# A two-block image kernel on one core: 64-channel halves on 128 partitions, decays further ahead, carry copies on GpSimd

## The reference, cut to what matters

```python
x = x + L0(_gn(x))      # B, C, H, W = 16, 192, 32, 32
x = x + L1(_gn(x))
# L0: projection to z (384), x (384), B, C (32 each), dt (12); depthwise 3x3 convolution and silu on x, B, C;
#     chunked scan (8 chunks of 128 tokens, 12 heads of 32) with att = (C B^T) * exp(cumsum) * dt;
#     layer norm, times z, output projection
# L1: projection to x_in (192), delta (192), B, C (16 each); softplus of delta; selective scan over 1024 tokens:
h = jnp.exp(d_t[..., None] * A) * h + (d_t * x_t)[..., None] * b_t[:, None, :]
y_t = jnp.einsum('bdn,bn->bd', h, c_t)
#     y + D * x_in, output projection
```

## Time and profile before

| | us |
|---|---|
| median of 3 runs | 3382.27 (3380.13 to 3385.87) |
| the profiled execution | 3382.05, span 3380.3 |
| TensorE busy | 2844.2 (84%) |
| VectorE busy | 2711.6 (80%) |
| ScalarE busy | 1929.9 (57%) |
| GpSimd busy | 1593.6 (47%) |
| granted TensorE clock, mean | 0.92 of full |

### The profile page before, as it was taken

One profiled execution on the slowest core, in us unless ns is written; L12 is line 12 of the kernel. 1 busy time (PEld: TensorE's weight loads), 2 busy tenths in 40 slices (PEclk: granted clock), 3 DMA queues, 4 the chain that ended last, 5 costly groups with the idle time before them and its releaser, 6 DMA issues. The chain is left out here.

```text
span 3380.3 us, 62242 instructions
## 1 busy us (share of the span) xinstructions
PE 2844.2 (84%) x20640; PEld 1502.5 (44%) x20640; DVE 2711.6 (80%) x4364; ACT 1929.9 (57%) x4507; POOL 1593.6 (47%) x1235
## 2 busy tenths in 40 slices
PE   3788888988888898888888888898888988888865
PEld 2554536353453634445354453544445354443510
DVE  1357979789697978979689797978969798797997
ACT  1637475564657547475664746547475664746542
POOL 2114545454454545545355444545545455554555
PEclk8989999899999989999899989989999999989976
DMA  2132141422314142241423215142241424214131
GB/s 52 25 99 70 60 139 49 131 73 86 97 54 137 54 129 78 68 123 54 120 73 106 82 50 140 51 141 73 74 109 54 119 73 123 79 58 128 42 113 59
DMA packets 104163, 290.97 MB, mean 86 GB/s; under 512 B 25373, under 2 KB 27020, under 8 KB 103820
## 3 DMA queue, kind: packets, MB, share of 16 engines
q1 hardware_dynamic: 103820, 286.71, 28.5%
HBM read 181.84 MB, written 39.85 MB: 66 GB/s over the span
## 5 line engine op out<-in xcount | busy, mean ns | idle before, releaser
L754 POOL TENSOR_TENSOR hc<-hst,bcrep 128x512 f32<-128x512 f32 x768 | 1202.0, 1565 | 1155.8 <-DVE hst L1249 1127.6
L1298 PE MATMUL bank<-hc,sel 128*32 128x512 f32 x1536 | 435.4, 650 | 113.3 <-POOL hc L754 109.5
L1236 DVE TENSOR_TENSOR wr<-durep,bcrep 128x512 f32<-128x512 f32 x768 | 520.1, 677 | 2.9 <-DMA bcrep<-bc_rows 2.9
L1249 DVE TENSOR_TENSOR_SCAN hst<-dec,wr 128x512 f32<-128x512 f32 x256 | 396.0, 1547 | 99.0 <-ACT carry L991 71.2
L842 ACT ACTIVATE ssd<-bank,ncs 128x128 f32<-128x128 f32 x1536 | 438.3, 385 | 48.7 <-PE bank L1298 47.0
L1298 PE MATMUL bank<-xna,wt0a 128*128 128x128 f32 (+3 forms) x1088 | 303.5, 381 | 46.0 <-DVE xnb L1056 27.6
L1249 DVE TENSOR_TENSOR_SCAN hst<-bank,carry,wr 128x512 f32<-128x512 f32 x240 | 306.4, 1277 | 22.7 <-ACT bank L950 13.3
L950 ACT ACTIVATE bank<-durep,aneg 128x512 f32<-128x512 f32 x368 | 251.3, 687 | 121.0 <-DVE hst L1249 63.3
L1298 PE MATMUL bank<-ssd,wcv 64*32 64x512 f32 (+1 forms) x6144 | 307.6, 543 | 0.0
L950 ACT ACTIVATE dec<-durep,aneg 128x512 f32<-128x512 f32 x400 | 290.3, 731 | 6.4 <-DVE hst L1249 4.7
L1298 PE MATMUL bank<-xnb,wt0b 128*128 128x128 f32 (+3 forms) x1088 | 289.3, 368 | 0.0
(11 more groups left out here) (189 smaller groups left out, 4975.3 us busy)
## 6 DMA issues: line engine op xcount, KB each, us to landing
durep<-scratch SPq DMA_DIRECT2D x192, 512.0 KB, 3.8
bcrep<-bc_rows SPq DMA_DIRECT2D x128, 512.0 KB, 4.9
ssd<-stage SPq DMA_DIRECT2D x384, 140.4 KB, 2.9
ssd<-bcst SPq DMA_DIRECT2D x128, 74.4 KB, 2.7
xa<-in_x_dram SPq DMA_DIRECT2D x16, 512.0 KB, 4.1
scratch<-u SPq DMA_DIRECT2D x32, 256.0 KB, 2.1
scratch<-delta SPq DMA_DIRECT2D x32, 256.0 KB, 2.5
out_dram<-x1a SPq DMA_DIRECT2D x16, 512.0 KB, 4.8
```

What stands on the lines that cost most here:

```text
L754: nc.gpsimd.tensor_tensor(hc[:, i % CRING, :], hst[:, i % HRING, :], bcrep[:, g, 1, :], ALU.mult).then_inc(hc_ready.sem, 1)
L1236: nc.vector.tensor_tensor(wr[:, i % WRING, :], durep[:, j % SLOTS_DU, 1, :], bcrep[:, g, 0, :], ALU.mult).then_inc(w_made.sem, 1)
L1249: nc.vector.tensor_tensor_scan(hst[:, i % HRING, :], decay_of(i), wr[:, i % WRING, :], carry[:, g:g + 1] if hf else 0.0, ALU.mult, ALU.add ...
L1298: return nc.tensor.matmul(out, lhsT, rhs, start=start, stop=stop, skip_group_check=True)
```

## The change

- **Halves on 128 partitions.** `xb`, `xnb` and `x1b` are 128 x 512 instead of 64 x 1024: the first half of the tokens on partitions 0 to 63, the second on 64 to 127. Weights for them are held twice. A pair of halves is then two matmuls over the first 128 channels and two of 64 rows each. One bn_stats goes for each set of statistics, and normalisation has half the elements a partition. `gb` is doubled and halved in value. The gate uses weights with zero rows (`wtz`).
- **Fills.** dt is projected with B and C (76 columns). VectorE adds the bias from the bank into `dtt`, TensorE turns it with four transposes (`step_lengths`), ScalarE copies it into `dtx`. Fills are eight, made in pairs.
- **Projections.** Both halves of a piece together, in slots 40 to 43, in the order dA, BC, xA, xdB; biases are added in ScalarE's copies (`p1b`).
- **Decays** are made two units further ahead up to unit 11 and one further ahead behind it; of the first eight, four have their home in SBUF.
- **Carry copies** go to GpSimd, behind the product with C. The dt additions stand behind VectorE's scan in slot 2.

```diff
-FILL_AT = (0, 0, 1, 1, 1, 1, 2, 2, 2)
-FILL_COPY_AT = (0, 0, 1, 1, 2, 2, 2, 3, 3)
+FILL_AT = (0, 0, 1, 1, 1, 1, 2, 2)
+FILL_COPY_AT = (0, 0, 1, 1, 2, 2, 3, 3)
-P1_AT = (4, 4, 5, 7, 7, 8, 9, 10)
+P1_AT = (4, 5, 6, 7)
+FRONT_UNITS, LEAD_UNITS = 8, 12
 def decay_bank(i):
-    if i < 8 or i >= 38:
+    if i < FRONT_UNITS:
+        return (0, 1, None, None)[i % 4]
+    if i >= 38:
         return i % 2
     return 6 + i % 2 if 31 <= i < 36 else None
+def decays_made(s):
+    return min(max(min(s + 3, LEAD_UNITS), s + 2), UNITS)
...
# GpSimd, states_by_c
+                if hf == 0:
+                    nc.gpsimd.tensor_copy(carry[:, i:i + 1], hst[:, i % HRING, HALF - 1:HALF]).then_inc(carried.sem, 1)
...
# ScalarE
+                if s == 3:
+                    act.wait_ge(dt_ps.sem, dt_ps.at(n, 1))
+                    by_half = bank[B_DT][:, :].rearrange("p (c h k) -> p h c k", c=CPH, h=2)
+                    for h in range(2):
+                        ins = nc.scalar.copy(dtx[:, h * CPH:(h + 1) * CPH, :], by_half[:, 1 - h, :, 0:NH])
+                    ins.then_inc(dtx_ready.sem, 1)
...
-                        decay(b, s, end, first)
+                        for i in range(decays_made(s - 1) if s else 0, decays_made(s)):
+                            decay(b, i, end, first)
...
-                        if 2 <= s < HU + 2:
-                            act.wait_ge(scanned.sem, scanned.at(b, s - 1))
-                            nc.scalar.copy(carry[:, s - 2:s - 1], hst[:, (s - 2) % HRING, HALF - 1:HALF]).then_inc(carried.sem, 1)
...
# VectorE, first_block_later
+                if s == 2:
+                    dve.wait_ge(fill_ps.sem, fill_ps.at(n, 6))
+                    for h in range(2):
+                        nc.vector.tensor_scalar(dtt[(1 - h) * CB_:(1 - h) * CB_ + NH, :], bank[FILL_BANKS[(4 + h) % 3]][2 * NS:2 * NS + NH, :],
+                                                dtb[2 * NS:2 * NS + NH, :], None, ALU.add).then_inc(dtt_ready.sem, 1)
...
# TensorE, fill
+                m, h = FILL_TILES[k]
+                c0, w = DI + m * P, P if m < XM else 2 * NS + NH
+                ps = [bank[FILL_BANKS[(k + h) % 3]] for h in range(2)]
+                for h in range(2):
+                    if k + h >= 3:
+                        pe.wait_ge(fill_copied.sem, fill_copied.at(n, k + h - 2))
+                    if k + h == 7:
+                        pe.wait_ge(dtt_ready.sem, dtt_ready.at(n, 1))
+                    mm(ps[h][0:w, :], wt0a[:, c0:c0 + w], xna[:, h * HALF:(h + 1) * HALF], True, False)
+                for h in range(2):
+                    rows = slice(h * CB_, (h + 1) * CB_)
+                    mm(ps[h][0:w, :], wt0b[rows, m * P:m * P + w], xnb[rows, :], False, True).then_inc(fill_ps.sem, 1)
+            def step_lengths(n):
+                pe.wait_ge(dtt_ready.sem, dtt_ready.at(n, 2))
+                pe.wait_ge(fill_copied.sem, fill_copied.at(n, 6))
+                for c in range(CPH):
+                    ins = nc.tensor.transpose(bank[B_DT][:, c * P:(c + 1) * P], dtt[:, c * Q:(c + 1) * Q], ident[:, :])
+                ins.then_inc(dt_ps.sem, 1)
...
# TensorE, conv
                 if u == 1:
+                    pe.wait_ge(dtx_ready.sem, dtx_ready.at(n, 1))
                     pe.wait_ge(fill_copied.sem, fill_copied.at(n, FILLS))
```

More of the change, by code:

```diff
@@ L94 @@
 MID = 1
-P1_TILES = (("dA", 0), ("BC", 0), ("xA", 0), ("xdB", 0), ("xdB", 1), ("dA", 1), ("xA", 1), ("BC", 1))
-K_BC, K_XA, K_MID, K_D2, K_X2 = 2, 3, 5, 6, 7
+P1_PIECES = ("dA", "BC", "xA", "xdB")
+P1_TILES = [(what, h) for what in P1_PIECES for h in range(2)]
+BIAS = {"dA": 0, "xdB": 1, "xA": 2, "BC": 3}
+K_D2, K_BC, K_XA, K_X2, K_MID = 2, 3, 5, 6, 8
 K_ALL = len(P1_TILES)
@@ L678, in _ @@
             made_before(nc.gpsimd.memset(mv[:, :, :], 0.0))
-            for t in stage + [bcst]:
+            for t in stage + bcst:
                 made_before(nc.gpsimd.memset(t[:, :], 0.0))
@@ L1630 @@
 EXP_LN = "natural_log_exp_and_others"
-NLOADS = 76
-PREPS = 12
+NLOADS = 79
+PREPS = 14
 DVE_STEPS = 35
```

251 lines of the change are left out of this document (128 added, 123 removed).

## The result

| | before | after |
|---|---|---|
| median | 3384.07 (4 runs, 3380.13 to 3385.88) | 3324.36 (4 runs, 3319.02 to 3333.08) |
| span of the profiled execution, us | 3380.3 | 3318.1 |
| TensorE busy, us | 2844.2 | 2745.2 |
| VectorE busy, us | 2711.6 | 2732.5 |
| ScalarE busy, us | 1929.9 | 1935.1 |

The ratio of after to before is 0.9828, with a 95% interval of 0.9801 to 0.9855, so 1.7% faster. The forecast was 3324.0. Three single executions that took far longer than the others of their kernel (3668.86 us of the kernel before, 5344.23 and 10289.23 in two of the experiments) are left out of all ratios and medians.

The account below looks back on a forecast made before the run. Bound: a chain along TensorE in the front, a ring through all engines in the chunk stage. From 3382.05 us, -73 - 9 + 22 - 4 + 6 = -58 gave 3324 us; 8 in 10 from 3283 to 3385.

Parts of the forecast that it names:

- The front: Normalisation to first convolution falls from 23.7 to 18.2 us, set by VectorE's dtt addition: net 73 us gained.
- The extra cost: Last matmuls before the first convolution at the lower clock in half the passes, 1.7 us each: 13 us lost.
- The sign that the prediction named: First convolution 18 to 19 us after normalisation in every pass, TensorE waiting ahead of it for VectorE's dtt addition.
- Rows to attention: Rows of chunk 0 to its attention: VectorE is ready when the chunk comes, 0.6 us a pass, 9 us gained.
- The 22.3 us: VectorE's waits for ScalarE's decays before the change, 1.4 us a pass, counted as a gain in the tail.
- Wind-down: Decays in slots 32 and 33 wait for scans ahead of the last chunk's normalisation: 1.45 us a pass, 22 lost.
- Tail: Slots 37 to 47: shorter decay waits against later u product and group variance, 4 us gained, bounds -25 to +25.
- Once: Start +4 us, first pass gains about 3, last pass pays 5 and last store 0.5: together +6 us.
- Rival 1: All of the front's gain arrives, clock up throughout, wait at slots 32 and 33 absorbed: 3289 us, chance 0.22.
- rival 2: Gain given back: dtt later, TensorE at 1.2 GHz in all passes, tail costs 25: 3370 to 3380 us, chance 0.15.
- Rival 3: Carry copy blocks GpSimd in the chunk stage, up to 1.67 us later in four slots: 3424 us, chance 0.12.
- Rival 4: Halves don't pair: each pair costs 0.86 us more, 3.4 a pass in the front: 3375 us, chance 0.06.

Follow-up runs that it names:

- the four runs with and without either cost: First convolution: changed kernel 18.79 us, matmuls added ahead of its fills 19.07, dtt additions inside its softplus 18.73 (3314.75 us total), both 17.96 (3314.12 us total).
- the added matmuls: The changed kernel with matmuls whose results nobody reads added in TensorE's idle time ahead of the fills: 3324.74 us, ratio 0.9821.
- the order swap: The changed kernel with ScalarE's decays of slots 32 and 33 behind the last chunk's normalisation and scaling, not ahead: 3309.61 us, ratio 0.9780.
- The last run but one: Changed kernel, dtt additions inside softplus, unread matmuls ahead of fills, group means and variances, decays of slots 32, 33 behind last chunk's work: 3244.53 us, ratio 0.9605.

## Why the prediction was right

**The front: right, with one cost in the wrong place.** The forecast was 18.2 us to the first convolution, set by the dtt addition behind the second softplus, and 0.9 us a pass on top for fills at half the clock; measured 18.79. The chain along VectorE was reckoned at 15.3 for the end of softplus 2, and it ended at 15.1. The halves pair, as the convolution's records promised. The extra cost was put on the last fills. It is on the first ones, in every pass. The fills were also reckoned too short: a pair of halves saves 0.47 us at the full level, not 0.86 (2.97 against four of 0.86), and B, C and dt cost 3.23, not 2.6. With both, TensorE's path came to have the length of VectorE's. That the two arrive together, so that neither alone sets the end, the prediction didn't see; the four runs with and without either cost show it. All passes came down to one line, 17.9 to 18.9, except the first of the 14 (22.2). The sign that the prediction named, TensorE waiting for the addition, shows only once its fills are faster, 0.89 us with the added matmuls. Two readings of the rows were off without consequence: the 12-column matmuls are 16, not 16 pairs, and the way from the first convolution to the rows of chunk 0 was 33.2 us in one pass, not 37.1 to 37.4.

**Rows to attention: the mechanism right, the size too small.** 0.6 us was taken from the first pass, which has no scans. Measured 1.62, and 1.05 more two attentions later, where the sum had nothing. The failed step was to give the gain to the carry copies alone: without them 0.64 is lost, without the lead of the decays and their homes in SBUF 1.43. These had been costed only for what they break, not for what they give: VectorE's scans run further ahead of the chunks. 37 us in 14 passes against 8. The 22.3 us that the prediction took for all waits for decays left out 18.1 for those in SBUF.

**Wind-down: the mechanism right, two terms missing.** 1.45 forecast, 2.63 measured, 1.72 of which the order swap gives back. The rows of after show the chain as reckoned: the scaling at 3.85 us behind the GpSimd result (1.4 in the swapped order). What the reckoning left out is, first, TensorE: it waits longer for ScalarE, and the gate matmuls then run at 1.2 GHz in 12 of 14 passes (0.63 us for two records, not 0.39), so the gate waits for them. In the two passes at the full level the last gate comes 1.3 us later than with the swapped order, so the order costs 1.3, near the 1.45, and the clock 0.4. Second, the layout: with decays and order as before the wind-down is 21.8, not 20.9, and the residual additions on partitions 64 to 127 account for it. Three of the four at 0.24 us and the start of the last at 0.11 make 0.84 of the 0.91 us, and with the swapped order VectorE falls behind the kernel before at exactly these places, step by step. No run undoes them, and why the upper partitions cost more isn't shown.

**Tail: wrong in sign, small.** +0.62 us, not -0.3. The sum weighed waits, and the tail is a chain of matmuls whose length is the granted clock: 3.5 or 5.8 us to the first projection. The last run but one shows that 4.1 us a pass lie there. Late first projections went from 5 to 7 of 14, which has the right sign; how much of the 0.62 that is, no run shows. The low level was there in the kernel before too: behind the wind-down of the earlier trace rows a window has it at 0.57.

```profile
1996.00:2010.00 14.00, 11.78 (x28) 5.36 (x30) 13.27 (x23) 0.92 (x2) 7.09 (x6) 0.57 0.40 132
```

The prediction priced the clock in the front alone.

**Once.** The first normalisation comes 8.0 us later, not 4. The last load lands 3.5 us later and the ScalarE copies from the first weight to the last constant take 11.6 us, not 6.8: each 64-row block is copied twice at 0.27 us, and in this stretch nothing covers them. The first pass gained 6.9 us, not 3, since its first convolution comes at 16.9 us instead of 22.7. The last stretch cost 1.4 with a pass of -4.6 in it, so the rest behind it paid about 6; 5.5 was forecast.

**The sum.** For 14 passes and what happens once: front -69 where -69 was forecast; rows to attention 2, -37 where -8; wind-down +37 where +20; tail +9 where -4; the stages without a forecast -4. The error of -29 at the chunks' start and those of +17 and +13 behind them cancel, which is luck: the first is the good side of the decays' lead, the second the residual additions and the clock, the third at least in part the clock. Rival 1 came in the front but for the clock; of rival 2 the low level came in all passes, but its price was covered by VectorE's path. Rival 3 is refuted by the period that doesn't move with copies taken away or doubled. Its upper price of 1.86 us is that of an operation held up for a scan and a product, and its lower one isn't that of an operation alone, as was written: while the multiplication of 0.19 us at 1986.03 ran, a scan from a bank was under way (1985.70 to 1986.98). So it isn't every scan that holds GpSimd up, and most copies took 0.18 or 1.11. Rival 4 is refuted by the records, and would have cost seven times what was put down.

## What to carry to other kernels

Price the granted clock wherever the critical path runs through short matmuls with gaps: four matmuls with unread results, in stretches in which TensorE idles anyway, gave 4 us a pass here, nearly as much as the whole change, and three of the four alone gave nothing. Where work is pulled ahead on an in-order queue, look at what its wait then stands in front of, and put it behind that in the few slots in which it matters. Where taking a cost off one path gives nothing, try it on both paths before calling either free, and read the gain at the end of the pass, not at the first event that moves. And when a tensor is laid out anew, compare each operation on it on the new partitions with the same one on the old.

## What the hardware showed

- TensorE can be busy for 31.86 of 33.77 us and be granted 1.2 GHz throughout, while matmuls of 128 rows alternate with lone ones of 64 rows. With the 64-row ones in pairs and the same matmuls otherwise, the level was full by 8.0 us behind normalisation in 13 of the 14 passes; in the first it fell again and was full from 15.9 on.
- The same residual addition of 64 x 128 elements costs VectorE 0.24 us more on partitions 64 to 127 than on 0 to 63 (0.64 against 0.40 us together with the one before it).
- Two 64-row matmuls on different rows of the array take the time of one (1.13 us for both at 2.4 GHz, 1.88 at 1.2). That holds also where both write one PSUM bank, to different partitions, as the B and C projection does: 1.05 us for both.

```profile
1978.31 1.05 PE L1341 MATMUL bank<-xnb,wt1b 64*32 64x512 f32 x4
```

  The Trainium skill, TensorEngine Tiling (Array Packing), section "Gotcha 1: PSUM Pressure", says that different row tiles can't access one bank at the same time; by this row they can here (one such matmul alone takes 1.04 us with the halves not side by side), and the 0.86 us a pass that the prediction left out of the sum isn't paid.
- A copy of one column takes GpSimd 648 ns in the mean and ScalarE 197. GpSimd's is 1.11 us or more in all 184 cases beside a VectorE scan with its decay in SBUF, and 0.18 in those beside a scan from a bank (2) or beside attention and like operations on a bank (62). It was worth moving there all the same, since nobody waited for it.
